# At the end of each batch's attention, the output product goes ahead of the next batch's projection

## What is computed

```python
x = x + attn(layernorm(x))        # 32 query heads, 8 key/value heads of 64, rope, alibi, tanh cap, causal
x = x + xattn(ctx_2048, ctx_2048, layernorm(x))
x = x + ffn(layernorm(x))         # ternary weights

# attn, cut to what matters
q, k, v = h @ Wq, h @ Wk, h @ Wv
q, k = rope(q), rope(k)
scores = 30 * tanh((q @ k.T + alibi) / 8 / 30)
ctx = softmax(causal(scores)) @ v
out = ctx @ Wo + bo
```

## Time and profile before

| what | value |
|---|---|
| median of three runs | 1186.9 us (1184.47 to 1188.2) |
| the profiled execution, its time | 1187.4 us |
| the profiled execution, its span | 1185.7 us |
| around the span | 1.7 us |
| mean granted TensorE clock | 0.994 |
| PE busy | 1148.9 us, 97% |
| DVE busy | 876.9 us, 74% |
| POOL busy | 700.1 us, 59% |
| ACT busy | 553.7 us, 47% |

### The profile page before, as it was taken

How to read it: one execution, slowest core, us unless ns; L and a number is a source line. 1 busy time by engine, 2 the same in 40 slices (tenths; PEclk the granted TensorE clock), 3 DMA queues, 4 the chain that set the end, 5 groups by cost and what they waited for, 6 DMA issues and landing times. The chain is left out here.

```text
span 1185.7 us, 24863 instructions
## 1 busy us (share of the span) xinstructions
PE 1148.9 (97%) x9730; PEld 794.2 (67%) x9730; DVE 876.9 (74%) x1286; ACT 553.7 (47%) x616; POOL 700.1 (59%) x565
## 2 busy tenths in 40 slices
PE   4879999999999999999999999999999999999998
PEld 3547556757656567576565677777886876786683
DVE  6777988788787887887877788888745644654654
ACT  6656665564764655637556500000244543542441
POOL 0475395694865956948659589999342422423331
PEclk9889999999999999999999999999999999999999
DMA  9445334553455345544454357773011022012000
GB/s 322 137 143 192 120 95 132 163 181 111 142 159 173 98 140 156 181 115 132 142 173 157 145 113 145 143 144 86 1 19 43 13 54 54 16 37 54 19 19 36
DMA packets 166142, 133.48 MB, mean 113 GB/s; under 512 B 69628, under 2 KB 127362, under 8 KB 166082
## 3 DMA queue, kind: packets, MB, share of 16 engines
q1 hardware_dynamic: 141128, 126.44, 36.1%
q10 hardware_dynamic: 24960, 6.29, 3.5%
HBM read 81.76 MB, written 35.21 MB: 99 GB/s over the span
## 5 line engine op out<-in xcount | busy, mean ns | idle before, releaser
L695 PE MATMUL bank<-hT_halves,w_hi 128*128 128x256 f16 x640 | 175.7, 274 | 6.2 <-DVE hT_halves L1410 4.8
L1963 POOL TENSOR_TENSOR parts<-parts 128x512 f32<-128x512 f32 x80 | 119.2, 1493 | 105.0 <-DVE parts L1426 104.9
L696 PE MATMUL bank<-hT_halves,w_hi 128*128 128x256 f16 x640 | 175.3, 274 | 0.0
L697 PE MATMUL bank<-hT_halves,w_lo 128*128 128x256 f16 x640 | 175.3, 274 | 0.0
L943 PE MATMUL bank<-kv,toep 128*128 128x288 f32 (+2 forms) x660 | 157.8, 401 | 0.7 <-ACT qT L1191 0.5
L1968 POOL TENSOR_SCALAR_AFFINE_SELECT region_c<-region_c 128x512 f32<-128x512 f32 x128 | 113.7, 912 | 55.7 <-ACT region_c L1157 55.7
L943 PEld LDWEIGHTS bank<-kv,toep 128*128 128x128 f32 x660 | 123.7, 190 | 34.0 <-ACT qT L1191 0.7
L1981 POOL TENSOR_TENSOR ctx_lo<-ctx,ctx_hi 128x512 f16<-128x512 f32 x64 | 99.3, 1552 | 59.4 <-ACT ctx_hi L1133 59.4
L2111 POOL TENSOR_TENSOR sqsum<-sqsum,toep 128x512 f32<-128x512 f32 x56 | 77.3, 1381 | 95.6 <-ACT toep L1333 95.5
L1154 ACT ACTIVATE region_c<-bank,cap_scale 128x1536 f32<-128x1536 f32 x64 | 98.7, 1543 | 70.3 <-PE bank L763 69.6
L1022 PE MATMUL bank<-odd_halves,guT 128*128 128x256 f16 x512 | 112.2, 273 | 0.0
(11 more groups left out here) (186 smaller groups left out, 2677.2 us busy)
## 6 DMA issues: line engine op xcount, KB each, us to landing
unit_halves<-halves SPq DMA_DIRECT2D x80, 256.0 KB, 2.2
q_both<-unit_halves SPq DMA_DIRECT2D x64, 256.0 KB, 2.9
q_high<-unit_halves SPq DMA_DIRECT2D x64, 128.0 KB, 3.0
toep<-kernel_padded SPq DMA_DIRECT2D x32, 256.0 KB, 4.0
wffn<-w_gu SPq DMA_DIRECT2D x6, 1280.0 KB, 6.2
cpair<-ctx_pairs SPq DMA_DIRECT2D x32, 176.0 KB, 4.8
xin<-x SPq DMA_DIRECT2D x8, 512.0 KB, 3.8
region_o<-wq SPq DMA_DIRECT2D x4, 1024.0 KB, 11.4
```

The lines of the kernel that those rows point to most:

```text
L695: pe.matmul(dst, lh, rh, start=first and k == 0, stop=False)
L696: pe.matmul(dst, lh, rl, start=False, stop=False)
L697: mm = pe.matmul(dst, ll, rh, start=False, stop=last and k == n - 1)
L1963: pool.tensor_tensor(slot[:, 0], slot[:, 0], slot[:, 1], ALU.add).then_inc(unit_summed, 1)
```

## The change

In the end part of `attend` on PE, the two statements of the loop body change places. Nothing else changes: the same instructions, the same waits, the same banks.

```diff
@@ -827,9 +827,9 @@
                 pe.wait_ge(tanh_done, NG * (b + 1))
                 left = range(STEPS - WO_AFTER, NG)
                 for n in range(EARLY):
-                    project(b + 1, n)
                     if n < len(left):
                         output(b, left[n])
+                    project(b + 1, n)
```

## The result

Over eight runs each, the changed kernel has a median of 1189.86 us (1188.8 to 1193.45) and the kernel before 1184.53 us (1183.24 to 1188.2). The ratio is **1.0039, 95% interval 1.0028 to 1.0050**: of 1184.5 us that is 4.6 us slower (the two medians stand 5.3 apart), where 3.4 were forecast.

The account below looks back on a forecast made before the run. PE bounds the loop, busy 78.47 of 78.7 us a batch. Batches 2 to 6 cost 5 x 0.4 = 2.0 us, batch 1 1.25, batch 7 0.15: 3.4 us, so 1190.3 us, range 1186.4 to 1194.2.

Parts of the forecast that it names:

- The hole: PE's wait for the DMA transposes ahead of P0 at each batch's end: goes, gaining 0.3 us a batch.
- O7 in batch 1: PE's output product O7 waits for POOL's late ctx_lo in batch 1: 0.85 us lost, once.
- P2 moves back, rotate 3 with it: On DVE at a batch's end, rotate 2 begins 2.27 us later, rotate 3 1.99 us late.
- DVE catches up in part, because of the lock: From rotate 3 to rotate 6, DVE's lateness falls from 1.99 to 1.0 us.
- the lock: DVE and POOL exclude each other on a shared SBUF port pair: low 3 waits for all of add 4.
- Rival B: DVE catches up wholly by rotate 6: not slower, -1.0 us in all, 1185.9 us; chance 0.18.
- rival C: DVE does not catch up between rotate 3 and high 6: up to 11.7 us slower, 1198.6; chance 0.16.
- case A: The walk holds: each batch costs 0.25 to 0.6 us, the sum 2.4 to 4.9; chance 0.66.
- high 6: ACT's last high unit of a batch's end: runs 299.01 to 299.63 in batch 2, 0.56 us late.
- sign of 79.5: Loop period above which the forecast is wrong in favour of rival C; 79.1 us was expected.
- The walk: Step-by-step timing of DVE, POOL and ACT from rotate 3 to high 6: cost 0.4 us a batch.
- Batch 7: The sums K0, waiting 0.40 us for POOL's key_sum, wait another 0.15 us.

Follow-up runs that it names:

- e1: Changed kernel with P2 put back ahead of O7, P0 and P1 still behind O5 and O6: ratio 0.9977 to the kernel before.
- e2: Kernel before with only P2 moved behind O7, P0 and P1 keeping their places: ratio 1.0053 to the kernel before.
- e3: Changed kernel with DVE's two output parts moved ahead of rotate 2: ratio 0.9993 to the kernel before.
- e9: Kernel before, with the lows at a batch's end reading one operand from PSUM and comparing (low halves left out): ratio 0.9988.
- e7: The changed kernel measured again, unaltered: ratio 1.0029 to the kernel before.
- e4: Changed kernel, with the lows at a batch's end reading one operand from PSUM and comparing instead of subtracting: ratio 0.9993 to the kernel before.
- e5: Changed kernel with a slot of its own for unit 6, so high 6 need not wait for unit 4's store: ratio 1.0019 to the kernel before.

## Why the prediction was right, and where it was short

- **The hole goes.** Right: none in the profile after, and 0.3 us a batch in e1 (78.40 for 78.70).
- **O7 in batch 1.** Right in kind and size: 0.89 for 0.85. That it came was partly luck: it is not there in each execution (e2, e3, e9 lack the lateness), and can come in another batch (e7). The forecast took it from one execution that happened to have it.
- **P2 moves back, rotate 3 with it.** Right, to 0.02 us. e1 and e2 show that this pair carries the whole cost.
- **DVE catches up in part, because of the lock.** Right: rotates 3 to 6 to 0.02 us. With the lock out of the way (e4, where the low halves are left out), rotate 6 came at 26.34 and the change became a gain in the loop. The Trainium skill, "SBUF — State Buffer", section "Who interferes with whom", says that a DVE instruction with two SBUF inputs contends with a GpSimd one that reads SBUF, and one with at most one SBUF input, outside DVE's 2-port modes, doesn't. The runs agree: 1.34 against 0.69.
- **Rival B** (all caught up) would have needed 78.4 a batch, **rival C** over 79.15. Most batches took 79.25: case A in its mechanism, near its upper end of 0.6 a batch in size, and just over C's line. Batch 2 (79.53, and 79.88 in e7) also passed the sign of 79.5 that was named for C, but by the wait for the store and not by C's lows. The time was within the range, and 4.6 us was in the half of A above 0.3%, though its interval begins at 0.28%. A's upper end of 4.9 us is more than its own terms give, 6 x 0.6 + 0.85 + 0.15 = 4.6; the loop's 4.85 lies between the two.
- **The term that was too small: high 6.** The walk had "high 6 299.01 to 299.63", right behind add 6. I had moved SP's stores and asked only whether units land in time for S0, not who waits for their slots. High 6 waits for unit 4's store: it began 0.56 after add 6 ended in batch 2, 0.3 in batches 3 to 5, and without the wait it is 0.11. Counted so, the store held high 6 up by 0.37, 0.45, 0.18, 0.17, 0.16 and 0.09 in batches 1 to 6, 1.4 us in all, and that is what the sum of 3.4 was short of. e5 takes the wait away and leaves 0.40 a batch, the walk's own 0.4; with the wait it is 0.57, and 0.82 in batch 2.
- **Two small readings at the walk's end cancel, by luck.** It let high 6 begin 0.03 after add 6, where the earlier trace rows and POOL's timeline have 0.11. And it let the tanh begin right at high 6's end. The 0.10 us between them in the earlier trace rows were read as all the slack there is, but there the tanh waits for S0; where it follows high 6, it begins 0.10 before high 6's end, so the slack was 0.2. In e5 the tanh begins at 30.91, the walk had 30.95. Nor was P7 without slack against the values: it begins 5.21 after S0 in the kernel before and in e1, in PE's own rhythm. Add 6 of batch 2 in the kernel before, 0.11 ahead of high 6 at 298.45:

```profile
296.70 1.64 POOL L1963 TENSOR_TENSOR parts<-parts 128x512 f32<-128x512 f32 x1 [0.98 <-DVE parts L1426]
```

- **Batch 7.** I had 0.15 for K0; its wait grew by 0.28, from 0.40 to 0.69. The span 6 to 7 is 0.75 longer, where 0.55 was forecast.

The sum: 1.25 + 4 x 0.4 + 0.55 = 3.4 forecast; 1.60 + 0.82 + 0.58 + 0.57 + 0.54 + 0.75 = 4.86 measured.

That the forecast time of 1190.3 us lies only 0.4 from the measured 1189.86 is luck too: the kernel before had a median of 1184.5 over eight runs and not the 1186.9 of the three, and that makes up for what the sum was short of.

## What to carry to other kernels

When a step moves back on the bound engine, look at what the engine behind it does between this step and the next: work that used to fill a wait (here 3.1 us of DVE's output) becomes lateness once the wait has moved ahead of it. Then follow the lateness to the first place with no slack, and ask at each step for its buffers too: a ring slot that had always been free in time became a wait here, when the store ahead of it went 1.8 us later and took 0.6 to 0.9 us longer to land. And a change of several like pairs is worth splitting: here two pairs gained 0.3 us a batch, and the third cost them and 0.6 more, so the version with the two alone (e1) is the one to keep.

## What the runs showed of the hardware

- A lateness of 0.7 us on DVE did not fade, though DVE had 0.7 us to spare for each unit. Where two rotates stood 1.9 or 2.1 us apart, POOL's add was ahead of DVE's next low, and the low took 1.30 and 1.48 instead of 0.68; where they stood 2.6 apart (the kernel before) or 3.2, DVE was first. So every second unit is late again (e3, batch 2). Without the second SBUF operand of the lows a lateness of 2.0 us at rotate 3 was down to 0.1 at rotate 6 (e4).
- A store that usually lands 2.2 us after its issue took 2.8 to 3.1 in the six batches of the changed kernel, issued 0.8 to 0.9 us behind the last of two other transfers of the same queue. In the kernel before the same store came 1.7 to 2.1 behind them and took 2.2 to 2.3. That the nearness is the cause was not tested.
- When PE stood idle, P7 began 0.06 us after the copy of the values had ended (303.30 to 303.36). Where PE was still at work, a copy that ended only 0.16 us before P7's turn cost it nothing (302.71 and 302.87 in the kernel before, the same distance in e1): the weight load had begun 0.05 after the copy, beside the matmuls ahead.
